# A four-block cross-attention chain: the third attention with its context products made ahead, and its softmax in one score pass

## The chip, the cores and the metric

The kernel runs on one core of a Trainium2 chip, one launch per call. The metric is the device time of one execution in microseconds (us), the whole chain from inputs in DRAM to the output. A core has five engines with a queue of instructions each: TensorE (PE; its weight loads are shown apart, as PEld), VectorE (DVE), ScalarE (ACT), GpSimd (POOL) and SyncE (SP), which here only starts DMAs. They meet at semaphores.

## The reference

x is 16 batches of 128 tokens of 256 channels, and passes through four blocks, each an attention over a context of 128 tokens per batch and then a feed-forward part, with LayerNorm ahead and a gated residual behind. The change is about the third attention:

```python
def _dyn_quant(x):
    s = jnp.maximum(jnp.max(jnp.abs(x), axis=-1, keepdims=True) / 127.0, EPS)
    q = jnp.clip(jnp.round(x / s), -127.0, 127.0)
    return (q, s)
...
def _w8a8_linear(x, w, b):
    qx, sx = _dyn_quant(x)
    qw, sw = _quant_weight(w)
    y = jnp.einsum('bnc,oc->bno', qx, qw) * (sx * sw[:, 0])
    return y + b
...
q = _w8a8_linear(x, wq, bq).reshape(B, N, H, D).transpose(0, 2, 1, 3)
k = (cond @ wk.T + bk).reshape(B, L, H, D).transpose(0, 2, 1, 3)
v = (cond @ wv.T + bv).reshape(B, L, H, D).transpose(0, 2, 1, 3)
scores = jnp.einsum('bhnd,bhld->bhnl', q, k) * inv_sqrt_d + mask[:, None]
attn = jax.nn.softmax(scores, axis=-1)
o = jnp.einsum('bhnl,bhld->bhnd', attn, v)
o = o.transpose(0, 2, 1, 3).reshape(B, N, C)
return _w8a8_linear(o, wo, bo)
...
x = x + jnp.tanh(g_xattn[2]) * _L2_xattn_ref(_layernorm(x, axis=-1), ctx_2048, mask_BxSxS2_ff0, ...)
```

There are 16 heads of 16 channels. k and v depend on the context alone, not on x. The chain's order is: attention 1, routed experts 1, attention 2, dense experts, attention 3, factor mix, attention 4, shared and routed experts.

## The kernel before, in words

x stays in SBUF for the whole run. The eight parts are eight stages, 0 to 7, run one behind the other; the third attention is stage 4. In a stage one batch is one turn, and each engine has a program of its own (`s4_sp`, `s4_pool`, `s4_dve`, `s4_act`, `s4_pe`), whose order of work is written out by hand; `turns` gives every turn b its neighbours pp = b−2, p = b−1, n = b+1 and m = b+2, so that a turn holds the score work of b, the values and output of batches before it, and the preparation of batches behind it. PSUM has eight banks of 512 columns; banks 4 to 7 hold the scores of one batch, 16 heads by 128 columns.

A turn of stage 4 before:

- **SP** loads the context of a batch and its mask twice, as it is and transposed (`load`, line 2538).
- **PE** makes the values (line 2792) and keys (2797) of batch n from the context, writes the mask into the score banks by products with an identity (`add_mask`, 2816, 8 matmuls of 512 columns, the mask in two parts that sum to it exactly), adds q·k for 16 heads (2874; each head's product contracts over 32 rows, so heads r = 0 to 3 sit in the four row groups of the array and banks 4 to 7). That is the first pass, laid out with queries on partitions, from which only each row's maximum is wanted.
- **DVE** takes the maxima (`TENSOR_REDUCE`, 2682), splits them in three bf16 parts (`split3`, lines 791 to 799).
- PE turns those (2887), ACT copies them (2745), and PE makes the scores a second time, now with keys on partitions: mask again (2816), minus the maximum through a selector product (2893), k·q (2898).
- **ACT** takes the exponentials, 1024 columns at a time (2765), and PE multiplies them with the values (2827). The values carry a column of ones, so the row sums come with them. PE turns the result (2835), DVE divides (2657, 2660) and quantises it (`quant`, 1263 to 1273, six steps), PE turns it (2841) and multiplies with the output weights (2847), DVE scales (2669), POOL adds bias and residual (`add_output`, 2587, 2589).
- For batch m, DVE takes LayerNorm's statistics (`ln_stats`, 759 and 762), POOL makes 1/sqrt (`rstd_step`, 775 and 777), DVE applies it (767) and quantises (`quantise_x`); for batch n, PE turns x (2786) and projects q (2803), DVE scales q and lays it out with zeros (`scale`, 2645 to 2649), PE turns it (2810), ACT copies it (2733).
- **POOL** also splits the masks (2580, 2582), and in the first two turns adds up factors for stage 5 (`add_factors`, 2604).

Ahead of stage 4, `stage_over` holds each engine until the stage before is done. Stage 1 (routed experts) begins with an exchange of rows through DRAM, so at the borders of stages 0, 1 and 2 PE waits for DMAs. Stage 3's programs begin in `s3_act.first()` (2111) with the conversion of its weights.

## Time and profile before

| | |
|---|---|
| Time, median of 3 runs | 1257.41 us (1252.7 to 1260.26) |
| The profiled execution | 1260.89 us, its span 1258.7 us |
| Mean granted TensorE clock, share of full | 0.939 |
| PE busy | 1057.4 us, 84% |
| DVE busy | 835.3 us, 66% |
| POOL busy | 551.9 us, 44% |
| ACT busy | 544.1 us, 43% |
| DMA | 112.72 MB, 90 GB/s mean |

How to read it: the span is the time from the first to the last instruction of the profiled execution; the rest of its time lies around it. Busy shares are averages over eight stages with different limits, so each question is put to the stretch it concerns. A group of instructions is named by line, engine, operation and the tiles it writes and reads; "x16" counts instructions.

### The profile page before, as it was taken

Reading aid. Unit: us, or ns where it says so; the run is one execution under the profiler, and the core shown is the slowest. Engines: PE = TensorE matmul, PEld = TensorE weight load, DVE = VectorE, ACT = ScalarE, POOL = GpSimd, SP = SyncE. Lnnn points to the kernel's source line nnn. Section 1 sums busy time; section 2 is a strip of 40 time slices with the busy share of each in tenths; the row PEclk is TensorE's granted clock in tenths of the full one; section 3 lists DMA queues with packets and bytes.
Section 4 is the critical chain, followed back from the end, with each engine's and each line's share of the span. In section 5 each row is a group of like instructions: output and inputs, shape, how many; then the busy total and the mean of one; then the engine's idle time right before and its main releaser. Section 6 shows DMA issues by size and latency. Waiting matters only on the chain.

```text
span 1258.7 us, 32458 instructions
## 1 busy us (share of the span) xinstructions
PE 1057.4 (84%) x11709; PEld 826.3 (66%) x11709; DVE 835.3 (66%) x2315; ACT 544.1 (43%) x1130; POOL 551.9 (44%) x1095
## 2 busy tenths in 40 slices
PE   4899898987388288889799899999978799789888
PEld 2576666665377244444577677777756589778888
DVE  3566665665555478887788868787765766555465
ACT  2455555554355267767211033333323444256432
POOL 2444555553787488861212252323233426500351
PEclk8899999999589779999899999999979999989999
DMA  5332333232367645542100000000022601134331
GB/s 186 98 98 78 111 102 104 87 123 88 105 196 212 158 123 144 154 121 83 67 1 1 17 26 27 17 25 17 9 64 75 196 2 64 72 118 152 101 99 62
DMA packets 107982, 112.72 MB, mean 90 GB/s; under 512 B 13132, under 2 KB 96292, under 8 KB 107596
## 3 DMA queue, kind: packets, MB, share of 16 engines
q1 hardware_dynamic: 98732, 88.47, 23.0%
q0 software_dynamic: 8256, 22.08, 5.9%
q8 instruction: 82, 1.34, 0.5%
q10 hardware_dynamic: 864, 0.43, 0.1%
q14 instruction: 48, 0.39, 0.1%
HBM read 66.09 MB, written 44.84 MB: 88 GB/s over the span
## 4 chain that ended last, share of the span: by engine, by line
PE 57%; DVE 18%; issue 9%; DMA 6%; ACT 4%; POOL 3%; SPq 2%; another core or an unknown queue 1%; ACTq 0%; DVEq 0%; POOLq 0%
PE psum L2816 5%; DMA PT<-xs 4%; PE psum L1102 3%; DVE mx L2397 2%; DVE x L2191 2%; DVE mx L872 2%; PE psum L2496 2%; PE psum L1701 2%; PE psum L1702 2%; PE psum L1034 2%; PE psum L1703 2%; PE psum L1065 2%; PE psum L1085 2%; PE psum L1070 2%; PE psum L1036 2%
## 5 line engine op out<-in xcount | busy, mean ns | idle before, releaser
L872 DVE TENSOR_REDUCE mx<-psum 128x6 f32<-128x960 f32 (+3 forms) x80 | 80.7, 1009 | 73.8 <-PE psum L1070 67.9
L775 POOL TENSOR_SCALAR veps<-mv 128x1 f32<-128x1 f32 x112 | 33.7, 301 | 206.3 <-DVE mv L762 148.3
L753 POOL DMA_INDIRECT got<-ys,rows_y x64 | 64.1, 1002 | 121.6 <-DMA ys<-yt 95.6
L959 ACT ACTIVATE PT<-psum 128x1024 f32<-128x1024 f32 x64 | 65.5, 1024 | 73.5 <-PE psum L1090 73.4
L2397 DVE TENSOR_REDUCE mx<-psum 128x4 f32<-128x1024 f32 x64 | 76.9, 1205 | 20.4 <-PE psum L2469 20.4
L2438 ACT ACTIVATE PT<-psum 128x512 f32<-128x512 f32 x128 | 69.5, 594 | 26.8 <-PE psum L2480 22.9
L1701 PE MATMUL psum<-xnTh,w7h 128*128 128x256 f32 x256 | 75.3, 294 | 1.6 <-issue 1.3
L1702 PE MATMUL psum<-xnTl,w7h 128*128 128x256 f32 x256 | 73.3, 286 | 1.0 <-issue 1.0
L1703 PE MATMUL psum<-xnTh,w7l 128*128 128x256 f32 x256 | 73.1, 286 | 0.9 <-issue 0.9
L2816 PE MATMUL psum<-mskp,ident_r 128*128 128x512 f32 x256 | 70.8, 413 | 2.9 <-ACT PT L2765 1.6
L2496 PE MATMUL psum<-PT,arena 128*32 128x256 f32 x1024 | 70.0, 389 | 0.0
L777 POOL TENSOR_TENSOR rstd<-veps,minus_half 128x1 f32<-128x1 f32 x112 | 64.1, 572 | 9.3
L1793 DVE TENSOR_TENSOR hTf<-sil,psum 128x256 f32<-128x256 f32 x64 | 26.8, 418 | 59.1 <-ACT sil L1775 41.8
L1775 ACT ACTIVATE sil<-psum 128x256 f32<-128x256 f32 x64 | 24.5, 385 | 88.4 <-PE psum L1703 73.7
L2191 DVE SCALAR_TENSOR_TENSOR x<-psum,cw,x 128x256 f32<-128x256 f32 x128 | 52.4, 476 | 12.6 <-PE psum L2073 12.3
L1912 PE MATMUL psum<-ident,PT 128*128 128x128 f32 x156 | 34.2, 305 | 31.1 <-DMA PT<-xs 29.8
L2071 PE MATMUL psum<-w3h,xnTh 128*128 128x512 f32 x128 | 53.3, 416 | 4.8 <-DVE x L2191 4.8
L2816 PEld LDWEIGHTS psum<-mskp,ident_r 128*128 128x128 f32 x256 | 45.0, 190 | 17.3 <-ACT PT L2765 5.8
L2011 DVE TENSOR_TENSOR xTl<-psum,xTh 128x256 fp32r<-128x256 f32 x78 | 33.1, 425 | 31.4 <-ACT xTh L1984 30.9
L2024 DVE TENSOR_TENSOR ht<-silt,psum 128x128 f32<-128x128 f32 x78 | 22.4, 287 | 44.4 <-ACT silt L1994 44.1
L1701 PEld LDWEIGHTS psum<-xnTh,w7h 128*128 128x128 f32 x256 | 49.7, 194 | 2.5 <-issue 2.5
L2072 PE MATMUL psum<-w3l,xnTh 128*128 128x512 f32 x128 | 50.7, 396 | 0.0
(431 smaller groups left out, 3403.9 us busy)
## 6 DMA issues: line engine op xcount, KB each, us to landing
xs<-qpad SPq DMA_DIRECT2D x34, 512.0 KB, 3.3
PT<-xs SPq DMA_DIRECT2D x78, 128.0 KB, 2.1
ys<-yt SPq DMA_DIRECT2D x78, 128.0 KB, 2.1
ctxT<-in_ctxT SPq DMA_DIRECT2D x48, 128.0 KB
ext<-qscr SPq DMA_DIRECT2D x96, 64.0 KB
arena<-in_w SPq DMA_DIRECT2D x16, 320.0 KB, 2.9
w_raw<-in_w SPq DMA_DIRECT2D x12, 384.0 KB, 3.5
q_parts<-kscr SPq DMA_DIRECT2D x66, 64.0 KB
```

Of the source, the lines that this page charges most:

```text
L753: pool.indirect_dma_start(out=dst[:, t % 4, k], out_offset=None, in_=ys[:], in_offset=bass.IndirectOffsetOnAxis(ap=rows_y[:, t, k:k + 1], ...
L777: nc.gpsimd.tensor_tensor(rstd[:, s], veps[:, s], minus_half[:], ALU.pow).then_inc(F("rstd").sem, 1)
L872: V.tensor_reduce(mx0[:, u0:u0 + m].rearrange("p j e -> p e j"), src, axis=AX.X, op=ALU.max, negate=True).then_inc(F("mx").sem, 1)
L959: A.activation(PT[:, 1024 * r:1024 * (r + 1)], bank(6, 2), ACT.Exp).then_inc(F("p").sem, 1)
L1701: MM(o, wh, xnTh[:, b % 2, c], start=(c == 0), stop=False)
L1702: MM(o, wh, xnTl[:, b % 2, c], start=False, stop=False)
L1703: t = MM(o, wl, xnTh[:, b % 2, c], start=False, stop=(c == NC - 1))
L2191: nc.vector.scalar_tensor_tensor(x[:, 2 * b + u], bank(2 + 2 * (j % 2) + u)[:, C * e:C * (e + 1)], cw[:, s, u, 2 * j + e:2 * j + e + 1], x ...
L2397: V.tensor_reduce(mx2[:, k // 2, 4 * (k % 2):4 * (k % 2) + 4], bank(4 - 4 * (k % 2), 2).rearrange("p (h l) -> p h l", h=4), axis=AX.X, op= ...
L2438: nc.scalar.activation(PT[:, 1024 * k + 512 * half:1024 * k + 512 * (half + 1)], bank(6 + half), ACT.Exp, scale=0.25).then_inc(F("p").sem, 1)
L2496: t = MM(bank(2 + s)[32 * m:32 * (m + 1), C * what:C * (what + 1)], g, PT[:, 1024 * k + 256 * m:1024 * k + 256 * (m + 1)], start=(k == 0 a ...
L2816: MM(bank(4 + r), ident_r[:], mskp[:, s, which, part].unsqueeze(1).to_broadcast([128, 4, T]), start=(part == 0), stop=False, skip_group_ch ...
```

## The change

- **Context products early.** k and v of all 16 batches are made by `context_pe` and `context_act` ahead of stage 4: batches 0 to 3 in the last turns of stage 0, 4 to 8 at the start of stage 1, 9 to 12 at the start of stage 2, 13 to 15 at its end. ACT copies them out of PSUM, starts the DMA that stores them in DRAM (`kvd`, 256 KB a batch) and the one that loads the context four batches on. Stage 4 loads them back (`load_kv`, four slots). In `s3_act.first()` ACT waits for all the stores.
- **One score pass.** Scores are made once, queries on partitions, in two halves (banks 4 and 5, then 6 and 7). DVE takes the maxima of each half, ACT makes the exponentials head by head with the negative maximum as bias (16 instructions of 128 columns in place of 2 of 1024), PE turns them (16 transposes), ACT copies them back (2 of 1024 columns). The selector, the split of the maxima, the second pass and the transposed mask are gone.
- **Who does what.** DVE takes over two copies from ACT (`copy_x`, `copy_values`). POOL takes over from DVE the LayerNorm application (`apply`), the rounding of x (`round_x`) and the laying of the values (`lay_values`). Quantising has five steps, not six.
- **The order of a turn** is new on every engine, and the loops are written out.

Cut to its core:

```diff
+        EARLY_PE = {NB + 1: (0, 1), NB + 2: (2,), NB + 3: (3,)}
+        LATER = {1: (4, 5, 6, 7, 8), 2: (9, 10, 11, 12), 3: (13, 14, 15)}
...
+                if i == NB + 2:
+                    act.wait_ge(loaded_later, LOADS_1)
+                    context_act(act, 0)
...
+        def context_pe(pe, k):
+            o, ct = bank(4 + k % 4), ctx_slot(k)
+            if k == 0:
+                pe.wait_ge(w_loaded[3], 32)
+            pe.wait_ge(ctx_in[k % 4].sem, ctx_in[k % 4].at(k // 4, 16))
+            if k >= 4:
+                pe.wait_ge(kv_copied.sem, kv_copied.at(k - 4, 1))
+            for c in range(NC):
+                nc.tensor.matmul(o[:, C:2 * C], ct[:, c], wvT[:, c], start=(c == 0), stop=(c == NC - 1), skip_group_check=True)
+            for g in range(2):
+                for c in range(NC):
+                    t = nc.tensor.matmul(o[:, 128 * g:128 * (g + 1)], wkT[:, c, g], ct[:, c], start=(c == 0), stop=(c == NC - 1), skip_group_check=True)
+            t.then_inc(kv_psum.sem, 1)
+        def context_act(act, k):
+            o, to = bank(4 + k % 4), stage_kv[:, k % 2]
+            act.wait_ge(kv_psum.sem, kv_psum.at(k, 1))
+            if k >= 2:
+                act.wait_ge(kv_stored[k % 2], 16 * (k // 2))
+            for g in range(2):
+                nc.scalar.activation(to[:, 128 * g:128 * (g + 1)], o[:, 128 * g:128 * (g + 1)], ACT.Identity, bias=bkc[:, g:g + 1])
+            nc.scalar.copy(to[:, C:2 * C], o[:, C:2 * C]).then_inc(kv_copied.sem, 1)
+            if k + 4 < NB:
+                act.dma_start(ctx_slot(k + 4), a["ctxT"][:, k + 4]).then_inc(ctx_in[k % 4].sem, 16)
+            act.wait_ge(kv_copied.sem, kv_copied.at(k, 1))
+            act.dma_start(kvd[k], to).then_inc(kv_stored[k % 2], 16)
...
+        def quant_scale(dve, src, sc, fl, item):
             V = nc.vector
             V.tensor_reduce(sc[:, 0:1], src, axis=AX.X, op=ALU.max, apply_absolute_value=True).then_inc(fl.sem, 1)
+            dve.wait_ge(fl.sem, fl.at(item, 1))
             V.tensor_scalar(sc[:, 1:2], sc[:, 0:1], 1.0 / 127.0, 1e-8, ALU.mult, ALU.max).then_inc(fl.sem, 1)
+            dve.wait_ge(fl.sem, fl.at(item, 2))
             V.reciprocal(sc[:, 2:3], sc[:, 1:2]).then_inc(fl.sem, 1)
+        def quant_round(V, eng, src, dst, sc, tmp, fl, item, k0):
+            V.tensor_scalar(tmp, src, sc[:, 2:3], MAGIC, ALU.mult, ALU.add).then_inc(fl.sem, 1)
+            eng.wait_ge(fl.sem, fl.at(item, k0 + 1))
+            if V is nc.gpsimd:
+                plain(eng)
+            V.tensor_scalar(dst, tmp, MAGIC + 127.0, MAGIC, ALU.min, ALU.subtract).then_inc(fl.sem, 1)
...
+                for u in range(2):
+                    act.wait_ge(kv_stored[u], 16 * (NB // 2))
...
+                if i < 0:
+                    for k in LATER[2][2 * (i + 3):2 * (i + 3) + 2]:
+                        context_act(act, k)
...
+            pe.wait_ge(kv_copied.sem, kv_copied.at(NB, 0))
...
+            def apply(m, s):
+                wait("rstd", m, 1)
+                if m >= 4:
+                    wait("xq", m - 2, 2)
+                P.tensor_scalar(xn[:, s, 0], x[:, m], mv[:, s, 0:1], rstd[:, s], ALU.subtract, ALU.mult).then_inc(F("xn").sem, 1)
+            def round_x(m, s):
+                wait("quant", m, 3)
+                wait("xT_psum", m - 1, 1)
+                quant_round(P, pool, xn[:, s, 0], qx[:], qsc[:, s], qt_p, F("xq"), m, 0)
...
+            def body(b, s):
+                pp, n, m = b - 2, b + 1, b + 2
+                if m < NB:
                     rs(m, s)
+                    apply(m, s)
+                if 0 <= pp < NB - 1:
                     add_output(pp)
+                if n < NB:
+                    split(n, 1 - s)
+                if m < NB:
+                    round_x(m, s)
+                if n < NB:
+                    lay_values(n, 1 - s)
+                if b < 2:
                     add_factors(4 * b)
...
+            def maxima(b, k):
+                wait("sq", b, k + 1)
+                V.tensor_reduce(mx4[:, 2 * k:2 * k + 2].rearrange("p r g -> p (r g)"), bank(4 + 2 * k, 2).rearrange("p (h l) -> p h l", h=8),
+                                axis=AX.X, op=ALU.max, negate=True).then_inc(F("mx").sem, 1)
+            def copy_values(p):
+                wait("pv", p, 1)
+                V.tensor_copy(bc_sb[:], bank(2)).then_inc(F("pvc").sem, 1)
...
+            def body(b, s):
+                pp, p, n, m = b - 2, b - 1, b + 1, b + 2
+                if b < NB:
+                    maxima(b, 0)
+                if n < NB:
+                    copy_x(n)
+                if m < NB:
                     ln_stats(4, dve, m, None, s)
+                if 0 <= pp:
                     output_scale(pp)
+                if n < NB:
                     scale(n, 1 - s)
+                if m < NB:
+                    wait("xn", m, 1)
+                    quant_scale(dve, xn[:, s, 0], qsc[:, s], F("quant"), m)
+                if 0 <= p < NB:
+                    copy_values(p)
+                if b < NB:
+                    maxima(b, 1)
+                if 0 <= p < NB:
+                    finish(p)
+                    quantise_o(p)
...
+            def exponentials(b, k):
+                wait("mx", b, k + 1)
+                if b > 0:
+                    wait("st", b - 1, k + 1)
+                for r in (2 * k, 2 * k + 1):
+                    for g in range(4):
+                        o = A.activation(p4[:, r, g], bank(4 + r)[:, 128 * g:128 * (g + 1)], ACT.Exp, bias=mx4[:, r, g:g + 1])
+                    o.then_inc(F("p").sem, 1)
+            def copy_p(b, k):
+                wait("st", b, k + 1)
+                if k == 0 and b > 0:
+                    wait("pv", b - 1, 1)
+                A.copy(pT4[:, 2 * k:2 * k + 2].rearrange("p r g q -> p (r g q)"), bank(4 + 2 * k, 2)).then_inc(F("mxT").sem, 1)
...
+            def scores(b, s, k):
+                if b > 0:
+                    wait("mxT", b - 1, k + 1)
+                if k == 0:
+                    wait("msk", b, 2)
+                    kv_loaded(pe, b)
                 for r in (2 * k, 2 * k + 1):
                     for part in range(2):
+                        MM(bank(4 + r).rearrange("p (g l) -> p g l", g=4), ident_r[:], mskp[:, s, part].unsqueeze(1).to_broadcast([128, 4, T]), start=(part == 0), stop=False, skip_group_check=True)
+                if k == 0:
+                    wait("qT", b, 1)
+                for g in range(4):
+                    for r in (2 * k, 2 * k + 1):
+                        t = MM(bank(4 + r)[:, 128 * g:128 * (g + 1)], qT4[32 * r:32 * r + 32, s, g], kv4[32 * r:32 * r + 32, b % 4, 128 * (g // 2):128 * (g // 2 + 1)], start=False, stop=True, skip_group_check=True)
+                t.then_inc(F("sq").sem, 1)
+            def transpose_p(b, k):
+                for r in (2 * k, 2 * k + 1):
+                    wait("p", b, r + 1)
+                    for g in range(4):
+                        t = nc.tensor.transpose(bank(4 + r)[:, 128 * g:128 * (g + 1)], p4[:, r, g], ident[:])
+                t.then_inc(F("st").sem, 1)
...
+            def body(b, s):
+                pp, p, n = b - 2, b - 1, b + 1
+                if b < NB:
+                    scores(b, s, 0)
+                if n < NB:
+                    transpose_x(n)
+                if 0 <= pp:
                     transpose_o(pp)
+                if 0 <= p < NB:
+                    transpose_p(p, 1)
+                if 0 <= pp:
                     output(pp)
+                if n < NB:
+                    project(n)
+                if 0 <= p < NB:
                     values(p, 1 - s)
+                if b < NB:
+                    scores(b, s, 1)
+                    transpose_p(b, 0)
+                if n < NB:
+                    transpose_q(n)
+                if 0 <= p < NB:
                     transpose_values(p)
```

PE's queue in one turn of stage 4 before (`mskp` is the mask, `k_parts` and `qT` are keys and queries, `mxq` the maxima with selector, `PT` the exponentials, `bc_sb` the values' product):

```order
L2816 MATMUL psum<-mskp,ident_r 128x512 x8
L2874 MATMUL psum<-k_parts,qT 128x128 x16
L2827 MATMUL psum<-PT,arena 32x128 x16
L2786 MATMUL psum<-identb,qx 128x128 x2
L2797 MATMUL psum<-ctxT,w_attn 128x128 x4
L2803 MATMUL psum<-qwT,qxT 128x256 x2
L2816 MATMUL psum<-mskp,ident_r 128x512 x8
L2887 MATMUL psum<-identb,mxp 48x128
L2835 MATMUL psum<-ident,bc_sb 128x128 x4
L2893 MATMUL psum<-mxq,w_attn 128x128 x16
L2810 MATMUL psum<-ident,qpad 128x128 x4
L2898 MATMUL psum<-qT,k_parts 128x128 x16
```

and the same turn now:

```order
L2929 MATMUL psum<-mskp,ident_r 128x512 x4
L2934 MATMUL psum<-arena,qT 128x128 x8
L2904 MATMUL psum<-identb,qx 128x128 x2
L2942 MATMUL psum<-ident,PT 128x128 x8
L2910 MATMUL psum<-qwT,qxT 128x256 x2
L2953 MATMUL psum<-arena 32x128 x16
L2929 MATMUL psum<-mskp,ident_r 128x512 x4
L2934 MATMUL psum<-arena,qT 128x128 x8
L2942 MATMUL psum<-ident,PT 128x128 x8
L2917 MATMUL psum<-ident,qpad 128x128 x4
L2962 MATMUL psum<-ident,bc_sb 128x128 x4
```

16 mask products became 8, 32 score products 16, and 16 selector and 6 context products went; 16 transposes of `PT` came. What is left stands in two halves, with other batches' work between them.

DVE's queue, from the scaling of q to the maxima, before:

```order
L2646 TENSOR_TENSOR arena<-psum,rows 128x16x16
L2649 TENSOR_TENSOR qpad<-q_tmp,rows 128x2x4x16 x2
L767 TENSOR_SCALAR xn<-x,mv,rstd 128x256
L1263 TENSOR_REDUCE qsc<-xn 128x1
L1265 TENSOR_SCALAR qsc<-qsc 128x1
L1267 RECIPROCAL qsc<-qsc 128x1
L1269 TENSOR_SCALAR qt_f<-xn,qsc 128x256
L1271 TENSOR_SCALAR qt_f<-qt_f 128x256
L1273 TENSOR_SCALAR qx<-qt_f 128x256
L759 BN_STATS stats<-x 128x6
L762 BN_AGGR mv<-stats 128x2
L2682 TENSOR_REDUCE mx<-psum 128x8 x2
```

and now, from the first maxima of a turn to the second (`bc_sb` is the values' product, `xres` the output):

```order
L2766 TENSOR_REDUCE mx<-psum 128x8
L2750 COPY qxT<-psum 128x256
L772 BN_STATS stats<-x 128x6
L775 BN_AGGR mv<-stats 128x2
L2795 SCALAR_TENSOR_TENSOR xres<-psum,osc,rows 128x256
L2756 SCALAR_TENSOR_TENSOR q_tmp<-psum,qsc,rows 128x256
L2759 TENSOR_TENSOR qpad<-q_tmp,rows 128x2x4x16 x2
L1318 TENSOR_REDUCE qsc<-xn 128x1
L1320 TENSOR_SCALAR qsc<-qsc 128x1
L1322 RECIPROCAL qsc<-qsc 128x1
L2771 COPY bc_sb<-psum 128x512
L2766 TENSOR_REDUCE mx<-psum 128x8
```

The three roundings of x and LN's application are gone from it. The maxima are two instructions with all of this between them. The start of x's quantisation (1318 to 1322) waits for `xn`, which POOL now writes.

POOL's queue in a turn now. Before, it held the 1/sqrt, the two additions of the output and the split, there of two masks at once:

```order
L788 TENSOR_SCALAR veps<-mv 128x1
L790 TENSOR_TENSOR rstd<-veps,minus_half 128x1
L2680 TENSOR_SCALAR xn<-x,mv,rstd 128x256
L2689 TENSOR_TENSOR xres<-xres,rows 128x256
L2691 TENSOR_TENSOR x<-x,xres 128x256
L2662 CAST mskp<-q_f 128x128
L2664 TENSOR_TENSOR mskp<-q_f,mskp 128x128
L1326 TENSOR_SCALAR rden<-xn,qsc 128x256
L1330 TENSOR_SCALAR qx<-rden 128x256
L2674 TENSOR_TENSOR arena<-arena,rows 128x16x16
```

Lines 2680 (LN's application), 1326 and 1330 (rounding of x) and 2674 (values) are the work it takes over.

## Rows read from the trace of the kernel before

**Rows 1.** The page, its first line.

```profile
span 1258.7 us, 32458 instructions
```

**Rows 2.** Windows: length; busy PE, PEld, DVE, ACT, POOL; clock; DMA share, GB/s.

```profile
455.00:590.00 135.00, 121.06 (x1412) 64.81 (x1408) 116.97 (x175) 95.94 (x162) 95.03 (x157) 0.99 0.47 133
...
731.00:917.00 186.00, 182.43 (x2379) 141.90 (x2379) 144.63 (x410) 69.36 (x134) 59.03 (x100) 1.00 0.07 19
```

**Rows 3.** Chain that ended last, one turn: start, us, what.

```profile
795.13 1.83 PE psum L2816 x8
...
798.61 0.44 PE psum L2810 x4
799.05 1.15 PE psum L2898 x32
...
800.22 1.03 ACT PT L2765
...
804.95 1.01 PE psum L2827 x32
...
806.18 0.95 PE psum L2797 x8
...
807.34 1.83 PE psum L2816 x8
```

**Rows 4.** Timeline of the same turn: start, us, engine, line, idle before.

```profile
794.95 0.63 ACT L2729 ACTIVATE k_parts<-psum,bkc 128x128 f32<-128x128 f32 x2 [0.28 <-PE psum L2797]
...
799.34 0.35 DVE L1269 TENSOR_SCALAR qt_f<-o_n,osc 128x256 f32<-128x256 f32 x1
...
800.83 0.73 POOL L2582 TENSOR_TENSOR mskp<-q_f,mskp 128x256 fp32r<-128x256 f32 x1
...
801.10 0.61 DVE L1269 TENSOR_SCALAR qt_f<-xn,qsc 128x256 f32<-128x256 f32 x1
...
803.85 0.57 POOL L777 TENSOR_TENSOR rstd<-veps,minus_half 128x1 f32<-128x1 f32 x1
```

**Rows 5.** Groups by line, DVE, the third attention (731 to 917 us).

```profile
L2682 DVE TENSOR_REDUCE mx<-psum 128x8 f32<-128x1024 f32 x32 | 37.7, 1220 | 16.2 <-PE psum L2874 16.2
L1271 DVE TENSOR_SCALAR qt_f<-qt_f 128x256 f32<-128x256 f32 x28 | 8.2, 294 | 1.0
...
L791 DVE CAST mxp<-mx 128x16 bf16<-128x16 f32 x15 | 3.2, 210 | 0.5
```

**Rows 6.** Line 2319, one operation on two engines: ns min/median/max.

```profile
L2319 POOL TENSOR_SCALAR xn<-x,mv,rstd x14: 1239/1244/1385, 441.9 to 560.6; 128x256 f32<-128x256 f32 x14
L2319 DVE TENSOR_SCALAR xn<-x,mv,rstd x2: 413/413/413, 429.3 to 434.1; 128x256 f32<-128x256 f32 x2
```

**Rows 7.** Groups by line and form, POOL.

```profile
L2604 POOL TENSOR_TENSOR kv_f<-kv_f,PT 128x512 f32<-128x512 f32 x7 | 8.9, 1275 | 0.5
```

**Rows 8.** The chain, start of the stage and start of the next.

```profile
724.35 2.07 PE psum L2797 x8
...
935.71 2.84 PE psum L2237 x8
```

**Rows 9.** Windows as in rows 2, at the first two borders.

```profile
324.60:336.80 12.20, 0.04 (x1) 0.00 (x0) 6.43 (x14) 0.00 (x0) 10.55 (x15) 0.50 0.24 76
420.00:440.50 20.50, 0.00 (x0) 0.00 (x0) 10.09 (x27) 2.15 (x5) 15.11 (x18) 0.56 0.89 186
```

**Rows 10.** The chain at the borders; the last two rows from the timeline.

```profile
420.25 0.43 SPq L2281
...
437.06 3.23 DMA ext<-qscr
...
597.76 2.07 PE psum L2496 x32
...
603.06 1.04 ACT L2115 CAST w3h<-arena 128x1024 fp32r<-128x1024 f32 x1 [4.40 <-POOL x L2340]
...
607.54 0.59 ACT L1362 COPY xnT<-psum 128x512 f32<-128x512 f32 x1 [3.43 <-PE psum L1356]
```

400 lines of the change are left out of this document (165 added, 235 removed).

## The prediction

> **What bounds the kernel now.** I read the page first, for the span, 1258.7 us [rows 1] of an execution that took 1260.89; then windows by stage, for the engine that has no idle time; then the chain of waits through one turn, for the pieces that make up its length; then groups and the timeline, for the price of one instruction. The stages run one behind the other, so what shortens stage 4 or lengthens a border shows in full. In the windows, stage 4 shows PE busy for 182.4 of 186 us at full clock, DVE 144.6, ACT 69.4, POOL 59.0 [rows 2]: there PE is the bound, and three engines have room. The chain says the same: nearly every piece of a turn is PE's, and one turn takes 807.34 − 795.13 = 12.21 us [rows 3]. Sixteen such turns lie between the stage's first row at 724.35 and stage 5's first at 935.71 [rows 8].
>
> **PE's turn.** A mask product of 512 columns costs 1.83/8 = 0.23, a 128-column transpose in f32 0.44/4 = 0.11, a full 128×128 f32 product 0.95/4 = 0.24, and the sixteen score products, four row groups at a time, 1.15, so 0.07 each [rows 3]. After the change: eight masks 1.83; sixteen transposes of the exponentials and eight others, 24 × 0.11 = 2.64; four bf16 ones, at most the same, 0.4; values 1.01 [rows 3]; two small projections, 0.46 by the mask product's price; and sixteen score products, now in halves that hold two row groups only. If two groups overlap as four did, a half is 8 × 0.24/2 = 0.96, both 1.92; if not at all, 3.84. I take the first, since the four groups of the row do overlap by 0.24/0.07, over three times. Sum 8.3 (10.2 without overlap). Keys, values, selector and second pass were the rest of 12.2, and they go.
>
> **ACT's turn.** No row has an exponential of 128 columns; the nearest is the key copy, an ACTIVATE with bias of that size. Two in a row take 0.63 [rows 4], so each one costs at least 0.27 and at most 0.36. Sixteen, in fours without a wait between them: 4.3 to 5.8, and I take the lower end, since they stand in a queue as the two do. The two copies of 1024 columns cost as much as the exponentials of that size, 1.03 [rows 3], a 512-column copy some 0.59 (the same form at 607.54 [rows 10]), the small one under 0.4. Sum 7.3, at most 8.8: not the bound by itself.
>
> **POOL's turn.** LN's application is in the trace on both engines, 1.244 us on POOL and 0.413 on DVE [rows 6]. The two roundings are TENSOR_SCALAR of the same shape, so 1.24 each. With the values and the two output additions as two-input operations of 128×256, 0.73 each (as the mask's line 2582), 1/sqrt 0.57 [rows 4] and its first step 0.2, the halved mask split 0.6: 3.72 + 2.19 + 0.77 + 0.6 = 7.3, and about eight waits between dependent instructions, 0.1 to 0.2 each by the gaps of such rows, so 8.3. In GPSIMD Engine Reference, § 4.1 Engine selection, the Trainium skill has POOL about 2× slower on two-input elementwise work and roughly at line rate on one input. By that the three TENSOR_SCALARs would cost 0.41 each, POOL's turn 5.8, and the time about 10 us less than mine. The trace disagrees by a factor of three, and the sum goes by the trace.
>
> **DVE's turn.** Busy is 144.6 × 12.21/186 = 9.5 [rows 2]. Out go the split of the maxima, 4 × 0.2; the three roundings of x, 0.61 + 2 × 0.29 [rows 4, 5]; LN's application and the laying of values, 0.41 each by its like [rows 6]; one step of o's quantising, 0.29: 3.1. In come two copies out of PSUM, 256 and 512 columns, 0.3 and 0.6 by the maxima's pace (1.22 for 1024). Maxima stay: 1.22 for each half [rows 5]. That is 7.3 of work, but with a new wait inside: after the statistics DVE goes on to the output scaling and q's scaling (1.4), then waits for POOL's `xn`, which takes 0.2 wake-up, 0.3, 0.57, 0.2, 1.24, 2.5 in all [rows 4, 6]. Exposed: 1.1. Behind this wait stand the values' copy, which PE's turn of values needs, and the second maxima, for which ACT waits. A further 1.0 I put on DVE waiting for PE ahead of maxima and `finish`. DVE's ring: 9.4. The other ring, scores, maxima, eight exponentials, transposes, copy, next scores, is 3.15 + 1.2 + 2.2 + 0.6 + 1.0 and semaphores, 8.5. With some blocking of DVE by POOL (below) I take **9.8 us a turn** against 12.2. Bounds: 9.3 with none of it, 11 if it is heavy.
>
> **The first three turns** carry stage 5's factor sums on POOL as before, seven of 1.275 [rows 7] and a split of about 2.3. They were free on a POOL that is busy a third of the time; now they stand in its queue: 3 × 8.3 + 8.9 + 2.3 = 36.1.
>
> **Stage 4.** Before, fifteen intervals between turns were 183.1. After: 12 × 9.8 + 36.1 = 153.7, so −29.4. The stage's head loses the key product of 2.07 [rows 8], of which a reload gives some back: −1.7. The end loses the last turn's 2.4 and about 2 of the second pass: −4.5. Together −35.6.
>
> **The borders.** The products, six matmuls and about 1.9 us of PE a batch at full clock (twice the keys' 0.95 [rows 3]), stand in stretches where PE does 0.04 of 12.2 us and 0.00 of 20.5 [rows 9], so PE's part is hidden, even at the granted clock of 0.50 that the row shows, the level of 1.2 GHz. What can surface is ACT's queue and the DMAs. *Stage 0 to 1*: ACT copies four batches, 1.0 each, and starts two DMAs each, 0.43 by SP's price [rows 10]; these stand ahead of stage 1's weight conversions and between the exponentials. DMA share is only 0.24 there. 0 to 5, I take 3. *Stage 1 to 2*: the DMA share is 0.89 over 20.5 us [rows 9], and the chain is on a 3.23 us transfer [rows 10]; four batches add 1.5 MB of which most moves later. 1 to 5, 2.5. *Stage 2 to 3*: PE's last product of the stage ends at 599.8; three context products at falling clock (1.9 each) then run to 605.5, and ACT waits for the last store, about 609.8 with copy and transfer. Its first conversion stood at 603.06, and its copy of 607.54 follows behind [rows 10]: late by about 3.5 (held to 609.8, two conversions-and-copies of 1.04 and 0.59 end at 611.6 instead of 608.1), of which a PE that never rested gives 1 back. 1 to 5, 2.5. Together +8. Stage 4's own loads, 256 KB a turn, have a DMA share of 0.07 around them [rows 2], hidden.
>
> **Sum:** −35.6 + 8 = −27.6. From 1260.9 that is 1233.3; the median of the runs lies 3.5 below the profiled execution, so **1230**.
>
> **Rivals.**
> *A, as forecast* (0.60): turn 9.5 to 10.1, borders +4 to +12; 1222 to 1238.
> *B, POOL and DVE block each other* (0.14). In the row, DVE's first rounding takes 0.61 while POOL's line 2582 runs (800.83 to 801.56), and ends 0.15 behind it; the same operation takes 0.35 with POOL idle [rows 4]. POOL was busy 0.32 of the stage and will be for 0.8, so most of DVE's SBUF operations meet it. At an extra 0.25 for each of five and as much for POOL, a turn is 11.0: 15 × 1.2 = 18 more, 1248. The Trainium skill, SBUF — State Buffer, § Who interferes with whom, says that of the two the one that comes second blocks fully until the first ends. The trace agrees (0.61 instead of 0.35).
> *C, two row groups don't overlap* (0.06): PE's turn 10.3, the ring with it, a turn 10.9: 12 × 1.1 + 1.1 = 14, 1244. For it: no row has two groups alone. Against it: the 0.07.
> *D, borders are free* (0.12): PE's idle stretches swallow all, and a PE that works in them is granted a higher clock after; turn 9.3. −6 − 6 = 1218.
> *E, the other side: the clock falls* (0.05). PE will be busy for 8.3 of 9.8. Where it rests, the granted clock is 0.50 [rows 9]. Should stage 4 drop to that level, PE's turn is 16.6, and the stage 15 × 16.6 = 249 against 183: with borders and ends about +66, 1325. It decides from four slow turns of sixteen on, which take back 4 × 6.8 = 27. Against it: stage 2 has PE busy 121 of 135, 0.90, at a clock of 0.99 [rows 2], not far from 0.85.
> *F, borders worse* (0.03): the added traffic at the second border is fully exposed, 1.5 MB at the window's 186 GB/s being 8 us, and the store wait delays stage 3 by 6.7; with B on top, −27.6 + 18 + 5.5 + 4.2, no change, 1257.
>
> **The numbers.** Likeliest 1230. A's range with B, C and the nearer halves of B and D gives 1215 to 1249; left out are E, F and the far tails, about 0.2. A measurement tells from no change about 0.5%, 6.3 us: faster means under 1251. A, C, D and two thirds of B: 0.87 faster. Same, 0.07: the rest of B, half of F. Slower: E and the worst of F, 0.06.
>
> **What would show it.** Stage 4's window about 175 us from first to last row, against 211; the interval between first mask products 9.8, with two kinds of turns alternating; PE busy about 0.85 of it at clock 1.00; POOL above 0.8; DVE idle before line 1318, released by POOL's 2680. In the first three turns, 10.7 to 12.9 each. Score halves near 0.96 each (1.9: C). DVE operations of 0.3 to 0.4 at 0.6 and above: B. Clock 0.5 in the stage: E. Stage 3's first conversion 5 to 7 us later relative to stage 2's end. The prediction is wrong if a turn is above 11 or below 9, or the borders together add more than 12.

## The result: 1245.3 us, a third of the forecast gain

| | before | after |
|---|---|---|
| Median of 6 runs | 1254.88 us (1252.66 to 1260.26) | 1245.30 us (1242.97 to 1247.22) |
| Ratio, 95% interval | | 0.9909 (0.9882 to 0.9936) |
| The profiled execution, its span | 1260.89, 1258.7 us | 1243.14, 1241.3 us |
| PE, DVE, ACT, POOL busy, us | 1057.4, 835.3, 544.1, 551.9 | 1048.9, 813.6, 597.3, 594.0 |

The kernel is faster by 9.6 us, 0.9%; 27.6 were forecast. The time lies in the range of 1215 to 1249, near its end, but the change is a third of the forecast one. The two profiled executions differ by 17.7 us, because the one of before was 6 above its median and the one of after 2 below.

The windows of the changed kernel, for the two borders of [rows 9] and for the steady part of stage 4, with the columns of [rows 2]:

```profile
324.60:336.80 12.20, 10.17 (x70) 9.49 (x69) 6.61 (x15) 7.37 (x19) 10.39 (x16) 0.97 0.66 213
420.00:440.50 20.50, 7.81 (x47) 6.52 (x46) 8.84 (x22) 6.21 (x19) 14.36 (x20) 0.75 1.01 221
772.00:904.00 132.00, 121.32 (x1348) 92.42 (x1347) 103.83 (x257) 91.70 (x262) 79.69 (x127) 1.00 0.09 25
```

The third attention has PE busy for 121.3 of 132 us, 0.92, at clock 1.00, against 0.98 before [rows 2]: less, but not the 0.85 of the forecast. The first border is no longer a rest for PE (10.17 us busy in 12.2, 0.04 before).

The chain of waits through one of its turns (start, us, what) answers to [rows 3]:

```profile
832.74 1.21 PE psum L2929 x4
833.95 1.09 PE psum L2934 x16
...
835.50 0.89 PE psum L2942 x8
...
836.41 1.02 ACT arena L2870
...
837.48 1.08 PE psum L2953 x32
838.56 1.12 PE psum L2929 x4
839.68 1.09 PE psum L2934 x16
840.77 1.04 PE psum L2942 x8
...
841.83 1.02 ACT arena L2870
...
842.90 1.21 PE psum L2929 x4
```

842.90 − 832.74 = 10.16 us a turn. Every piece is PE's but two: twice PE has turned the exponentials of a half (L2942), and ACT copies them out of PSUM (L2870, 1.02 us) before PE may go on, to the values (L2953) or to the next masks in the same banks (L2929). DVE and POOL aren't on it.

I cut the traces at the same places: the last work on x of each stage, and the first masks of each turn. The head of stage 4 is what lies ahead of its first masks, the tail what lies behind the first masks of its last turn, up to the last work on x.

| stretch, us | before, two traces | after | forecast change | measured |
|---|---|---|---|---|
| end of stage 0 to PE's start of stage 2 | 127.4, 123.4 | 126.7 | +3 and part of 2.5 | +1.3 |
| stage 2 | 162.5, 163.5 | 165.3 | rest of 2.5 | +2.3 |
| end of stage 2 to end of stage 3 | 121.3, 121.2 | 128.1 | +2.5 | +6.9 |
| stage 4, head | 4.1, 4.1 | 2.9 | −1.7 | −1.2 |
| its first three turns | 36.2, 35.8 | 36.7 | −0.5 | +0.6 |
| its twelve next turns | 12 × 12.22 | 12 × 10.17 | −28.9 | −24.6 |
| its last turn and tail | 24.1, 24.1 | 24.9 | −4.5 | +0.8 |
| stages 5 to 7 | 322.9, 323.3 | 322.3 | 0 | −0.8 |

The second trace of before is that of run b0 below; the measured column is against the mean of the two. These stretches add up to −14.7. Stage 0, which is not in the table, took 312.0 against 313.1 and 317.7, another −3.4; that makes the −18 between the spans (1241.3 against 1258.7 and 1259.9). The medians of the runs say −9.6, so this pair of traces shows more gain than most executions have, and what lies between the two is not placed; the first row is the one that varies most between traces (below). The stretches miss the forecast by 27.6 − 14.7 = 12.9, and three places make up 14.0, of which other rows give 1.1 back: the turns (4.3), the tail (5.3) and the border of stages 2 and 3 (4.4).

That border in the timeline (start, us, engine, line; the second fence is the DMA view of 597 to 619 us, to landing):

```profile
606.33 0.36 SPq L3165 DMA_DIRECT2D PT<-in_w  x1
...
607.20 0.33 ACTq L1313 DMA_DIRECT2D kvd<-xnT  x1
...
615.38 1.04 ACT L2178 CAST w3h<-arena 128x1024 fp32r<-128x1024 f32 x1 [8.21 <-DMA kvd<-xnT]
```

```profile
PT<-in_w SPq DMA_DIRECT2D x1, 2048.0 KB, 8.6
kvd<-xnT ACTq DMA_DIRECT2D x3, 256.0 KB
```

ACT starts the last store at 607.20. 0.9 us ahead of it, SP has started the load of stage 5's factors, 2 MB in 8.6 us; it waited only until PE had made the last product. ACT, which waits for the store, starts stage 3 at 615.38, 8.21 us idle, where I had put 609.8. The packets of the trace show how the store was held: the load moves in 128 packets of 16 KB, 0.61 us each in the median, from 607.3 to 614.5, and the store in 128 packets of 2 KB, 0.08 us each, the first at 611.1 and the last until 614.9.

### The profile page after: what moved, and what is told of

It is laid out like the page before. It is cut to its first block, busy times and chain, and to the rows that moved or that the text cites. A ratio compares the mean times of both kernels' runs of the same rounds, so it can differ in the third digit from the quotient of the medians.

```text
span 1241.3 us, 30784 instructions
## 1 busy us (share of the span) xinstructions
PE 1048.9 (84%) x11053; PEld 818.5 (66%) x11053; DVE 813.6 (66%) x2192; ACT 597.3 (48%) x1354; POOL 594.0 (48%) x1153
## 3 DMA queue, kind: packets, MB, share of 16 engines
q1 hardware_dynamic: 96892, 89.65, 23.7%
## 4 chain that ended last, share of the span: by engine, by line
PE 54%; DVE 19%; issue 9%; DMA 6%; ACT 6%; POOL 4%; SPq 1%; another core or an unknown queue 1%; ACTq 0%; DVEq 0%; POOLq 0%
PE psum L1125 3%; DMA PT<-xs 3%; PE psum L2929 2%; DVE mx L2465 2%; DVE x L2259 2%; PE psum L2934 2%; PE psum L2942 2%; DVE mx L888 2%; PE psum L2569 2%; ACT arena L2870 2%; PE psum L1057 2%; PE psum L1758 2%; PE psum L1108 2%; PE psum L1760 2%; PE psum L1059 2%
## 5 line engine op out<-in xcount | busy, mean ns | idle before, releaser
L2863 ACT ACTIVATE PT<-psum,mx 128x128 f32<-128x128 f32 x256 | 70.0, 395 | 9.0 <-DVE mx L2766 9.0
L2259 DVE SCALAR_TENSOR_TENSOR x<-psum,cw,x 128x256 f32<-128x256 f32 x128 | 52.4, 476 | 12.5 <-PE psum L2134 12.2
L2870 ACT COPY arena<-psum 128x1024 f32<-128x1024 f32 x32 | 32.4, 1012 | 45.6 <-PE psum L2942 45.6
L1250 POOL COPY arena<-kv_f 32x64 f32<-32x64 f32 x160 | 38.7, 242 | 27.4 <-POOL arena L1250 22.1
L2134 PE MATMUL psum<-w3h,xnTl 128*128 128x512 f32 x128 | 50.6, 395 | 0.0
```

Source lines behind the costliest of these rows:

```text
L2259: nc.vector.scalar_tensor_tensor(x[:, 2 * b + u], bank(2 + 2 * (j % 2) + u)[:, C * e:C * (e + 1)], cw[:, s, u, 2 * j + e:2 * j + e + 1], x ...
L2863: o = A.activation(p4[:, r, g], bank(4 + r)[:, 128 * g:128 * (g + 1)], ACT.Exp, bias=mx4[:, r, g:g + 1])
```

## The experiments

Eleven runs were made, in three groups (a0, e1, e2, e3; b0, e4, e5, e6; c0, e8, e7), each group beside the kernel before on one chip. That chip isn't the same for all: the kernel before has a median of 1237.2 in the first group, 1258.7 in the second and 1239.2 in the third. The traces of the changed kernel place it in two ends of the program in about equal parts: stage 0 ends at 312.0 us in its first trace and at 303.1 and 302.6 in a0 and c0, and stage 7, which no kernel here touches, takes 249.9, 240.4 and 238.7. So times are compared within a group, and stretches of stages 2 to 4, which agree across groups to about a microsecond, across all. The changed kernel ran in the first and third group only; in the second, a time can be held against before alone.

### The two kernels again: how much a trace varies

> The changed kernel itself, once more, as the measure for the three kernels that run beside it. Its profiled execution was 17.7 us under that of before, while the medians of six differ by 9.6 only. Theory 1 (the profiled execution of before was a long one): this trace again shows a turn of 10.2 us in the third attention, 36 us for its first three turns, and a time of 1243 to 1247. Theory 2 (the changed kernel itself varies by several us between executions, by its DMAs at the borders): the turn is the same, but the stretch from the end of stage 0 to the first product of stage 2, 126.7 us in the first trace, is off by 3 us or more.

> The kernel before itself, for a second trace. Its first profiled execution took 1260.89, six runs have a median of 1254.9. Theory 1 (that execution was a long one, in the transfers at the borders): the third attention again takes 211 us and stage 7's programs the same as before, and the stretch from the end of stage 0 to the first product of stage 2, 127.4 us in the first trace, is 3 to 6 us shorter; then the changed kernel's 126.7 to 128.3 there is a loss, where by the first pair of traces it looked free. Rival (borders 1 and 2 are free): it is 127 again.

> The changed kernel again, as the measure for the two beside it. Expected: turn 10.15 to 10.2, third attention 185 to 187 us, stage 3's first conversion 11 us behind the end of stage 2, ratio to before 0.99.

The changed kernel (a0 and c0): 1227.9 and 1229.6 us, ratios 0.9900 (0.9866 to 0.9934) and 0.9927 (0.9901 to 0.9954); turns of 10.17 and 10.18, stage 4 185.5 and 186.9. The kernel before (b0): one execution, 1262.1 us, stage 4 210.6. From the end of stage 0 to stage 2 it took 123.4, 4.0 less than in the first trace, as theory 1 of that run had it, although its time is no shorter, since stage 0 was 4.6 longer. Theory 1 of a0 holds for the turns and the first three of them (36.9), and its stretch was 128.3, 1.6 more than in the first trace and not 3; over all traces below it does differ by more than 3. So one pair of traces says little about the first two borders. Over the ten traces of changed kernels with all context products, this stretch takes 126.7 to 131.1, mean 128.8, against 125.4 for the two of before: the products cost 3.4 there, and with 2.5 in stage 2 and 6.5 at the third border (127.7 in the mean of the changed kernel's three), 12.4 in all. Both traces of before leave the third border at 121.2, so that part is firm. Stage 4 gives 24.6 back (186.3, the mean of the changed kernel's three, against 210.9), which leaves 12.2, where the three pairs of medians say 9.3 to 9.6. These 3 us have no place in the stretches.

### One store behind a 2 MB load

```diff
-                sp.wait_ge(kv_psum.sem, kv_psum.at(NB, 0))
+                for u in range(2):
+                    sp.wait_ge(kv_stored[u], 16 * (NB // 2))
                 sp.dma_start(factors, a["w5"]).then_inc(w_loaded[5], 16)
```

> Edit: SP starts the 2 MB load of stage 5's factors only when all context products are stored, no longer when PE has made the last. Theory 1 (the last store, started at 607.20, queues behind the 2 MB load started at 606.33, and ACT, which waits for it, starts stage 3 at 615.38): the store lands at about 609.5 (2.3 us for 256 KB), stage 3's first conversion is 5.5 to 6 us earlier relative to the end of stage 2, and the time is 5 to 6 us less than that of the changed kernel. Rival (the store is slow by itself, and my forecast of 609.8 was too low for that reason): the conversion moves by less than 1 us and the time does not change.

1223.2 us (e1) against 1227.9 for the changed kernel in its group, 4.7 less; the two ratios to before, 0.9891 (0.9858 to 0.9924) and 0.9900 (0.9866 to 0.9934), overlap, so it is the trace that decides. The timeline of this kernel at the border:

```profile
597.34 0.33 ACTq L1313 DMA_DIRECT2D kvd<-xnT  x1
...
599.43 0.36 SPq L3166 DMA_DIRECT2D PT<-in_w  x1
599.45 1.04 ACT L2178 CAST w3h<-arena 128x1024 fp32r<-128x1024 f32 x1 [2.14 <-DMA kvd<-xnT]
```

Store started at 597.34, landed at about 599.4, 2.1 us, where it had taken 8.2; its packets run from 598.2 to 599.0, and SP's load now starts behind it. From the end of stage 2 to ACT's first conversion it is 5.3 us, 11.0 in the changed kernel beside it: 5.7 less, in the middle of what theory 1 gave, and the whole stage 3 ends that much earlier (121.9 against 127.8). The rival is out. With a store of 2.1 us the first trace would have had it at 607.20 + 2.1 = 609.3, near my 609.8. Then the third border costs 0.7 (121.9 against 121.2), less than the 2.5 of the forecast.

### Copies by bank: PE's two waits

```diff
-                A.copy(pT4[:, 2 * k:2 * k + 2].rearrange("p r g q -> p (r g q)"), bank(4 + 2 * k, 2)).then_inc(F("mxT").sem, 1)
+                for r in (2 * k, 2 * k + 1):
+                    wait("st", b, r + 1)
+                    A.copy(pT4[:, r].rearrange("p g q -> p (g q)"), bank(4 + r)).then_inc(F("mxT").sem, 1)
```

with PE's transposes signalled bank by bank, its masks waiting for their own bank, and its values starting with three of the four copied.

> Edit: the turned exponentials are copied out of PSUM bank by bank (4 copies of 512 columns in place of 2 of 1024), each as soon as its four transposes are done, and PE's next masks and values wait for their bank only. Theory 1 (PE's order is the bound: 9.3 us busy in a turn of 10.2, and the rest is PE waiting at the two copies, 0.5 ahead of the values and 0.2 ahead of the masks): the two waits go almost wholly, a turn is 9.4 to 9.6, 12 us x 0.65 = 8 us less. Rival B (DVE and POOL block each other, and DVE's queue with its 1.3 us wait for xn is what holds the turn): the turn stays at 10.1 to 10.2 and PE's wait only moves, to the maxima's or exponentials' side.

1219.9 us (e2), 8.0 less than the changed kernel, as much as theory 1 gave, but not where it gave it, and with ratios that touch (0.9856, 0.9808 to 0.9904, against a0's 0.9866 to 0.9934). Stage 4 is 8.0 shorter too (177.4). A turn takes 9.79, 0.38 less and not 0.65; twelve make 4.6. The tail lost 2.4 to 3.6 (21.4), part of it to a higher granted clock and not to the edit (see the tail below); the first three turns lost 1.3. The waits tell why a turn stopped at 9.8. PE, 780 to 880 us, the changed kernel of this group and then this one (engine, line, waited for: us in total, times, longest):

```profile
PE psum L2953 <- ACT arena L2870: 5.3, 10, 0.5
PE psum L2929 <- ACT arena L2870: 2.3, 10, 0.2
```

```profile
PE psum L2930 <- POOL mskp L2664: 2.7, 10, 0.4
PE psum L2971 <- DVE qo L1330: 2.1, 9, 0.2
```

The waits for ACT are gone, and new ones for POOL's masks and DVE's rounding have come. The chain now runs through these two alone:

```profile
821.47 1.25 POOL xn L2680
...
823.54 0.59 DVE bc_sb L2771
824.13 1.13 DVE mx L2766
...
827.22 0.69 DVE qo L1330
827.91 1.13 DVE mx L2766
...
829.72 0.19 DVE mv L775
...
830.42 0.58 POOL rstd L790
...
831.30 1.24 POOL xn L2680
```

From one `xn` (821.47) to the next (831.30) is 9.83 us: values' copy, second maxima, o's quantising, first maxima, statistics, POOL's 1/sqrt and `xn`. That is the ring that the forecast had at 9.4, and took at 9.8. It was there, and a PE ring of 10.16 lay over it. That its length meets the forecast so well is in part luck: per turn DVE is busy for 7.9 us (7.3 forecast) and waits 1.4 for `xn` (1.1), while it never waits for PE's scores or values, for which 1.0 was put in; the rest is gaps between dependent steps.

### LayerNorm's application back on DVE

```diff
                     rs(m, s)
-                    apply(m, s)
```

on POOL, and `ln_apply` in its place on DVE, ahead of the quantising of x.

> Edit: LayerNorm's application of x goes back from POOL (1.24) to DVE (0.41) in the third attention; all else as in the changed kernel. Theory 1 (PE's order with its two copies is the bound, and DVE's 1.3 us wait for xn costs nothing): the turn stays at 10.1 to 10.2 and the time within 2 us. My forecast's theory (DVE's ring, 9.4, is the longest): DVE's wait shrinks by 0.8, and a turn is 0.5 or more shorter.

1243.3 us (e6), beside 1258.7 for before, a ratio of 0.9875 (0.9814 to 0.9936) that the changed kernel's 0.9909 also lies in; a turn takes 10.02, 0.15 less. The stage takes 182.8, 3.5 shorter; the first three turns give 2.2 and the next twelve 1.8. So in the changed kernel the longer way of `xn` costs a turn 0.15, a little more than theory 1's nothing and far from the 0.5 of the other. It is different with both edits.

### Both together

> Edit: e2 (copies by bank) and e6 (LayerNorm's application on DVE) together. Copies by bank alone gave a turn of 9.83 with PE busy 9.3, and its chain of waits ran through DVE and POOL only (maxima, o's quantising, statistics, POOL's 1/sqrt and xn, back to DVE's quantising of x, values' copy, maxima). The application alone gave 10.02. Theory (with PE's two waits gone, the DVE and POOL ring is the bound, and the application's 1.24 on POOL against 0.41 on DVE is part of it): a turn is 9.4 to 9.5, PE's own busy time, and the stage 5 to 8 us shorter than e2's 177.4. Rival (after e2 PE is the bound already, and 9.83 is its work with gaps): the turn stays at 9.8.

1212.5 us (e8), 17.1 less than the changed kernel beside it (1229.6). A turn takes 9.21, a little under what the theory gave, and stage 4 168.7, 8.7 shorter than e2's. The rival is out. The windows view of 760 to 860 us in e7, which has the same turn:

```profile
760.00:860.00 100.00, 98.33 (x1137) 77.28 (x1138) 92.77 (x229) 77.21 (x239) 68.30 (x109) 1.00 0.11 32
```

PE is busy for 98.3 of 100 us, and the waits of e8 show none of PE's in that stretch. 9.2 is PE's own work, and a bound for this order and these instructions. One edit gave 0.38, the other 0.15, both 0.96: two rings of nearly one length, of which each hides the other's gain. The application's move does two things at once: `xn` comes sooner, and POOL no longer works beside DVE's two rounding steps of o, which take 0.35 and 0.29 in e6 and e8 and took 0.41 and 0.66 in e2. How the gain divides between the two no run shows.

### Where POOL's additions run

```diff
-                if b < 2:
-                    add_factors(4 * b)
+                if 1 <= b < 12:
+                    if b < 9:
+                        add_factors(b - 1)
```

with one addition in each call, and the split of the bias in turn 11.

> Edit: POOL adds one of stage 5's factors in each of the turns 1 to 8, and splits the bias in turn 11, in place of four and four additions in turns 0 and 1 and the split in turn 0. Theory 1 (the first three turns, 36.3 us, are bound by this work in POOL's queue; in a later turn POOL is busy 6.1 of 10.2 and has room for 1.28 more): the first three turns take about 31, the others stay at 10.2, and the time is 4.5 to 5.5 us less than that of the changed kernel. Rival (POOL's queue as a whole bounds a turn): nine turns lengthen by up to 1.3 each and the time is the same or more.

1227.3 us (e3), no gain. The first three turns fell to 29.8, a little more than said, but the seven turns behind them, one for each addition, took 11.1, seven times 0.92 more. In the changed kernel POOL stands idle for 2.69 us of a turn at that place (ahead of line 788 at 837.37), so the queue has room. What the addition met was DVE:

```profile
795.51 1.31 POOL L2702 TENSOR_TENSOR kv_f<-kv_f,PT 128x512 f32<-128x512 f32 x1
795.73 1.24 DVE L1330 TENSOR_SCALAR qo<-qt_f 128x256 bf16<-128x256 f32 x1
```

DVE's rounding took 1.24 us, 0.29 elsewhere, and ended at 796.97, 0.15 behind POOL's addition (795.51 + 1.31 = 796.82). If that is all, it is enough to start the addition behind it:

```diff
                 if 1 <= b < 12:
+                    wait("oquant", b - 1, 5)
                     if b < 9:
```

> Edit: as e3 (one factor addition in each of the turns 1 to 8, the split in turn 11), but POOL waits ahead of it until DVE has rounded o (semaphore of line 1330), so that the addition runs beside DVE's maxima, which read PSUM. In e3 those turns took 11.09 in place of 10.15, with DVE's line 1330 at 1.24 in place of 0.29, ending 0.15 behind POOL's addition. Theory 1 (the addition cost its turn 0.93 because DVE's rounding was blocked by it): the turns are back at 10.15 to 10.3, the first three take 31 in place of 37, and the time is 4.5 to 5.5 less than that of the changed kernel. Rival (POOL's queue is too full for 1.28 more): the turns 1 to 8 stay at 11 or get longer, since the addition now starts later.

```profile
806.13 0.29 DVE L1330 TENSOR_SCALAR qo<-qt_f 128x256 bf16<-128x256 f32 x1
...
806.60 1.27 POOL L2702 TENSOR_TENSOR kv_f<-kv_f,PT 128x512 f32<-128x512 f32 x1 [0.66 <-DVE qo L1330]
```

The addition starts at 806.60, behind DVE's rounding of 0.29, and runs beside the maxima, which read PSUM. The turns with an addition are back at 10.1 to 10.3, and the first three take 33.4 (36.9 in two traces of the changed kernel, 36.7 in the first). The stage is 2.6 us shorter (183.7), not 5, because turn 0 took 12.9 here and 9.7 in e3 (below); the time (e4) was 1243.4 against 1258.7 for before, a ratio of 0.9863 (0.9799 to 0.9928), which alone tells nothing against the changed kernel's. The rival, a queue too full, is out: the same 1.28 us of work costs a turn 0.92 or nothing, by what it runs beside.

### What the context products cost

```diff
+            if k >= 4:
+                nc.tensor.matmul(o[:, 0:128], wkT[:, 0, 0], wkT[:, 0, 1], start=True, stop=True, skip_group_check=True).then_inc(kv_psum.sem, 1)
+                return
...
-                sp.dma_start(kv4[:, b % 4], kvd[b]).then_inc(ctx_in[b % 4].sem, 16)
+                sp.dma_start(kv4[:, b % 4], kvd[b % 4]).then_inc(ctx_in[b % 4].sem, 16)
```

and ACT's copies likewise.

> Edit: keys and values are made, stored and loaded for batches 0 to 3 alone, each used for four batches; of the products of batches 4 to 15 only a small matmul and one or two small copies stay, to keep the counts. What it leaves out: 12 of 16 batches' context products, their stores and their context loads. Theory 1: stage 3's first conversion stands at the end of stage 2 again (11 us less), the first product of stage 2 comes 1 to 3 us earlier, stage 2 is 1 to 3 us shorter; together the borders' price is 12 to 16 us of the changed kernel's time, and the time is so much less. Rival (only the wait for the last store costs anything, the rest of the products is hidden): 8 to 11 us less, all of it at stage 3's start.

1228.4 us (e5), 15.0 less than e4 and e6 beside it (1243.4), which are 1.8 and 2.8 us ahead of e5 in stage 4; so by the medians these products cost about 17. ACT's first conversion stands 0.03 us behind stage 2's end again, stage 2 takes 162.6 (165.5 with all products, the mean of ten traces), and the stretch ahead of it 125.0 (128.8). Of the 11 us that ACT waited, stage 3 had given back 3.6, since other engines prepared it meanwhile; to its end it is 7.4 less. 2.9 + 3.8 + 7.4 = 14.1. Theory 1 holds by the stretches (12 to 16), and its rival is out: the products cost something at all three borders, and half of it is the last. The first border is the least firm, one trace of e5 against ten that differ by 4.4. By the medians the price is some 3 us above the stretches, as with the 3 us that had no place above.

### All mends

e1, e2, e4 and e6 together, and

```diff
-                for u in range(2):
-                    act.wait_ge(kv_stored[u], 16 * (NB // 2))
                 for j in range(4):
                     if j == 1:
+                        for u in range(2):
+                            act.wait_ge(kv_stored[u], 16 * (NB // 2))
                         front(0, 0)
```

> Edit: e1, e2, e4 and e6 together, and ACT waits for the context stores only ahead of its first copy into their buffer, behind its first conversion. Theory (three causes that do not overlap: PE's two waits and DVE's ring in the turns, POOL's factor additions in the first turns, the last store behind the 2 MB load): the third attention takes 168 to 172 us (turns 9.4 to 9.5, the first three 30 together), stage 3's first conversion stands at the end of stage 2 and its first copy 5 us behind, and the time is 20 to 24 us less than that of the changed kernel, a ratio to before of 0.970 to 0.976. Rival (the mends share one gain, or the borders take it back): less than 14 us.

**1205.0 us** (e7; 1202.8 to 1208.2), a ratio to before of **0.9719** (0.9686 to 0.9752), 24.7 less than the changed kernel beside it: 0.7 over the end of what was expected. Stage 4 takes 168.1, its turns 9.23, the first three 31.5; from the end of stage 2 to that of stage 3 it is 120.2, a little under the kernel before. Two details were missed: the turns are shorter than the 9.4 to 9.5 expected and the first three longer than 30, and stage 3's first conversion stands 3.5 us behind the end of stage 2, since ACT still copies the last context products there (its first copy is 5.2 behind, as expected). This version beats both kernels by clear margins: 34.2 us under the kernel before, more than the 27.6 that the forecast saw in the change as it was.

## Why the prediction was wrong

**Direction and place were right**: the gain is in stage 4's turns, the price at the borders, POOL's application costs 1.24, eight exponentials in a queue 2.19 (0.27 each, as taken), and the DVE and POOL ring is 9.8. Two halves of scores took 1.09 each (0.96 forecast), 0.14 for a product where one that stands alone has 0.24, so two row groups do overlap, and rival C fell. The clock in the steady part of the stage was 1.00, and E fell. The first three turns came to 36.7 beside 36.1, but that is luck: POOL is busy for 26.7 of these 36.65 us, and the chain is on it only from 741.11 to 756.73, behind PE and ahead of DVE. POOL's own turn was put at 8.3 and is 6.1 busy. That the additions lengthen these turns e3 and e4 show.

27.6 forecast, 9.6 measured, has these steps in it:

**"Sum 8.3 … Keys, values, selector and second pass were the rest of 12.2, and they go."** PE's work in a turn is 9.2. Masks cost 1.12 to 1.21 for four, 0.29 each and not 0.23; scores 2.18 and not 1.92; transposes of `PT` 1.93 and not 1.76; the small ones make up the rest. The trace of before had a nearer price for masks (2.18 for eight) beside the one that I took. In the chain of [rows 3] eight stand in a row for 1.83, and later in the same turn two groups of four:

```profile
801.29 1.21 PE psum L2816 x4
...
802.64 0.97 PE psum L2816 x4
```

After the change all masks come in fours between other work.

**"DVE's ring: 9.4. The other ring … 8.5."** The failure of method. I laid out two rings, one of DVE and one from scores to next scores, and took the longest. I did not lay out PE's own queue with its waits inside it: each half's copy, 1.02, has only 0.5 to 0.9 of PE work behind it that doesn't need it, so a turn of 10.16 is PE busy for 9.35 (121.32/132 of it) and some 0.8 of waiting, 0.5 ahead of the values and 0.2 ahead of the masks. e2 shows it: the waits go, and what comes up is 9.8, the forecast's number. 12 × 0.36 = 4.3 us.

**"The end loses the last turn's 2.4 and about 2 of the second pass: −4.5."** It grew by 0.8. The chain there:

```profile
901.62 1.23 DVE mx L2766
902.85 1.29 DVE xn L780 x4
...
906.03 0.30 DVE qo L1330
...
906.77 1.72 PE psum L2942 x8
...
908.52 1.02 ACT arena L2870
...
909.58 1.98 PE psum L2953 x32
...
911.58 0.70 DVE bc_sb L2771
...
912.33 1.13 PE psum L2962 x4
```

For the last batch there is no other work to lay over the new steps. Maxima of the second half, stage 5's LayerNorm (1.29, which stood there before too, 1.30), o's quantising of the batch before, transposes, copy and values come one behind the other. All from the transposes on is at half the clock, 0.50 granted from 905.5 us to the end (before, from 924.2, for 11.3 of 24.1 us): 1.72 for eight transposes (0.89 in a turn) and 1.98 for the values (1.08). One pass less was given for a longer string. I had taken off a full turn's saving where the engines don't overlap. The tail's length goes with the granted clock. The windows of the tail in the changed kernel, in its second trace (a0), in e2 and in e8:

```profile
893.80:918.72 24.92, 16.45 (x156) 12.09 (x157) 16.79 (x50) 11.42 (x32) 5.96 (x12) 0.74 0.00 1
886.96:910.70 23.74, 15.27 (x156) 11.30 (x157) 16.78 (x50) 11.42 (x32) 5.95 (x12) 0.84 0.00 1
883.48:904.83 21.35, 14.25 (x159) 10.32 (x158) 16.81 (x50) 11.79 (x36) 5.94 (x12) 0.91 0.00 1
873.88:896.48 22.60, 15.49 (x159) 11.37 (x158) 16.95 (x50) 11.87 (x36) 5.92 (x12) 0.83 0.00 1
```

The same kernel has 24.9 at a mean clock of 0.74 and 23.7 at 0.84. The copies by bank are to be compared at one clock: 22.6 in e8 (0.83) and 22.9 in e7 (0.84) against 23.7, so they are worth about 1 us; the 21.4 of e2 has the clock in it as well. The rest is read from the rows only.

**"The last store, about 609.8."** It landed at 615.3, and ACT went on at 615.38. The 2 MB load that SP starts at the same event was in the diff (`kv_psum.at(NB, 0)` ahead of the factors), and I asked only what the context's own traffic would meet, not which transfer is released just ahead of the one that is waited for. e1: 5.7 us, more than the whole 4.4 by which this border missed; with the store alone it costs 0.7. The first two borders, 5.5 forecast in all, cost 3.4 + 2.5.

**Rival B** was right in its mechanism and wrong in its place. DVE's first rounding of o takes 0.60 on average, 0.35 before, since POOL lays the values then. The Trainium skill's rule (SBUF — State Buffer, § Who interferes with whom), that where an operation of each wants the port pair that the two share, the one that comes second blocks fully, agrees with e3: 1.24 in place of 0.29, ending 0.15 behind. The operation alone takes 0.29, so a part of it seems not to be held. But in the changed kernel's steady turns this lies under PE's ring, and the chain shows none of it. In its third turn, beside POOL's additions, it does: DVE's two steps stand on the chain at 760.79 and 761.73 with 0.92 and 1.31. It decides where an addition of 1.3 us comes in (e3), and it is part of e2's ring, where the second step of o's rounding stands with 0.69.

## What to carry to other kernels

Lay out every engine's own queue with its waits in it, above all the one that is busiest, and ask behind each wait what work stands there that doesn't need it. Take the price of an instruction from a row where it stands as it will stand: the masks in fours were in the trace. A bank that is written, read, and written again by the same engine through another needs the other's copy to be covered, or cut in pieces. Before a wait for a DMA is put on a path, look which large transfer is released by the same event. And when a mend gives half of what it should, look for a second ring of nearly the same length before dropping it. Two tails are compared only at the same granted clock.

## What the runs showed that I had not expected

- **POOL's TENSOR_SCALAR has no one price.** Three of 128×256 in f32, by line and form, 772 to 904 us:

```profile
L2680 POOL TENSOR_SCALAR xn<-x,mv,rstd 128x256 f32<-128x256 f32 x11 | 13.6, 1238 | 3.4 <-POOL rstd L790 3.4
L1330 POOL TENSOR_SCALAR qx<-rden 128x256 bf16<-128x256 f32 x12 | 12.9, 1077 | 2.6 <-POOL rden L1326 2.6
...
L1326 POOL TENSOR_SCALAR rden<-xn,qsc 128x256 f32<-128x256 f32 x11 | 5.3, 482 | 1.1
```

1.24 with two operands per partition, 1.08 with two constants and a bf16 result, 0.48 with one operand and a constant. I had taken 1.24 for all. POOL is so busy for 6.1 of a turn, not 7.3. Of what GPSIMD Engine Reference, § 4.1 Engine selection, in the Trainium skill says of one-input work, roughly line rate, the third is near (DVE has 0.35 for it), the other two are not.
- **Turn 0 has two lengths**, 9.8 and 12.9 us, and they go with the granted clock at its start: 0.84 over the first ten microseconds in the first trace of the changed kernel, 0.50 in its third (c0):

```profile
735.00:745.00 10.00, 8.02 (x59) 6.07 (x59) 4.78 (x13) 3.98 (x11) 3.14 (x6) 0.84 0.07 26
```

```profile
725.30:735.30 10.00, 8.80 (x47) 6.34 (x46) 4.21 (x13) 2.75 (x9) 2.85 (x6) 0.50 0.00 0
```

All eleven traces of changed kernels follow it: 9.4 to 9.8 in the five where these ten microseconds have 0.83 to 0.86, and 12.3 to 12.9 in the six where they have 0.50. What decides which of the two comes isn't shown. The first three turns of the changed kernel came to nearly the same sum either way (36.7 and 36.9), so it shows only where that is mended.
- **Work put into PE's idle stretch held its clock** (0.97 where it was 0.50, in the first window above), but from the end of stage 0 to stage 2 the time did not fall: 126.7 to 131.1 us in ten traces, 123.4 and 127.4 before.
